# A two-expert mixture kernel's routing tables: one-hot tables for all eight experts, or for two with the rest scattered as 64-byte records

## The reference, cut to what matters

```python
logits = xf @ gate_w.T                       # xf: the rotated tokens, 4096 x 512
scores = softmax(logits); topv, topi = top_k(scores, 2)
gates = topv / topv.sum(-1)
# place of a token in its expert: running count over first choices, then second; valid below cap = 1024
flat_idx = where(valid, topi * cap + loc, 0)
disp[flat_idx] += xf * w                     # w = valid
h = relu(de @ fc1_w[e].T + fc1_b[e])         # 1024 x 512 by 512 x 2048, for each e
eo = h @ fc2_w[e] + fc2_b[e]                 # 1024 x 2048 by 2048 x 512
out = x + (eo[flat_idx] * gates * w).sum()   # over the two choices
```

## Time and profile before

| | |
|---|---|
| median of 3 runs | 1422.17 us (1420.65 to 1422.97) |
| the profiled execution's own time | 1426.31 us |
| its span in the trace | 1424.3 us |
| mean granted TensorE clock | 0.989 of full |
| PE busy | 1377.4 us, 97% of the span |
| DVE / ACT / POOL busy | 74% / 50% / 22% |

### The profile page before, as it was taken

One profiled execution on the slowest core, in us unless ns is written; L12 is line 12 of the kernel. 1 busy time (PEld: TensorE's weight loads), 2 busy tenths in 40 slices (PEclk: granted clock), 3 DMA queues, 4 the chain that ended last, 5 costly groups with the idle time before them and its releaser, 6 DMA issues.

```text
span 1424.3 us, 18010 instructions
## 1 busy us (share of the span) xinstructions
PE 1377.4 (97%) x6154; PEld 1129.6 (79%) x6154; DVE 1058.2 (74%) x1598; ACT 705.1 (50%) x1056; POOL 310.6 (22%) x322
## 2 busy tenths in 40 slices
PE   8488999999999999999999999999999999999997
PEld 5367888888888888888888888888888888888885
DVE  6897879686886778686896878777796868855443
ACT  5445445545464455554464445554455454644442
POOL 1054303321025202241033201251032200220021
PEclk9799999999999999999999999999999999999999
DMA  8666575566466564476466564575555533543232
GB/s 293 234 161 154 117 153 154 166 121 150 91 188 156 119 127 133 142 162 137 92 178 164 106 139 117 156 170 132 99 170 145 114 78 67 153 120 68 51 109 67
DMA packets 448684, 194.15 MB, mean 136 GB/s; under 512 B 398432, under 2 KB 400617, under 8 KB 446674
## 3 DMA queue, kind: packets, MB, share of 16 engines
q1 hardware_dynamic: 426466, 125.98, 40.0%
q0 software_dynamic: 22128, 67.03, 15.1%
HBM read 153.21 MB, written 39.98 MB: 136 GB/s over the span
## 4 chain that ended last, share of the span: by engine, by line
PE 93%; DVE 2%; ACT 1%; DMA 1%; issue 1%; POOL 1%; another core or an unknown queue 0%; SPq 0%; POOLq 0%; ACTq 0%
PE ps L1210 15%; PE ps L1206 15%; PE ps L1214 15%; PE ps L1181 14%; PE ps L1182 14%; PE ps L1183 14%; PE ps L1126 1%; PE ps L1198 1%; PE ps L1197 1%; PE ps L1199 1%; PE ps L1108 1%; PE ps L1109 1%; DMA x_all<-in_x 1%; POOL h L371 0%; DMA h<-in_x,gather_row 0%
## 5 line engine op out<-in xcount | busy, mean ns | idle before, releaser
L1181 PE MATMUL ps<-yc_hi,w1c_hi 128*128 128x512 f32 x896 | 350.2, 391 | 4.2 <-ACT s L606 2.2
L1182 PE MATMUL ps<-yc_lo,w1c_hi 128*128 128x512 f32 x896 | 349.4, 390 | 0.0
L1183 PE MATMUL ps<-yc_hi,w1c_lo 128*128 128x512 f32 x896 | 349.2, 390 | 0.0
L1206 PE MATMUL ps<-w_hi,h_hi 128*128 128x512 f32 x952 | 254.4, 389 | 0.0
L1210 PE MATMUL ps<-w_hi,h_lo 128*128 128x512 f32 x952 | 254.4, 389 | 0.0
L1214 PE MATMUL ps<-w_lo,h_hi 128*128 128x512 f32 x952 | 254.4, 389 | 0.0
L1206 PEld LDWEIGHTS ps<-w_hi,h_hi 128*128 128x128 f32 x952 | 178.7, 188 | 37.1
L1214 PEld LDWEIGHTS ps<-w_lo,h_hi 128*128 128x128 f32 x952 | 178.7, 188 | 37.1
L1210 PEld LDWEIGHTS ps<-w_hi,h_lo 128*128 128x128 f32 x952 | 178.7, 188 | 37.0
L1181 PEld LDWEIGHTS ps<-yc_hi,w1c_hi 128*128 128x128 f32 x896 | 168.5, 188 | 43.1 <-ACT s L606 2.6
L1183 PEld LDWEIGHTS ps<-yc_hi,w1c_lo 128*128 128x128 f32 x896 | 168.6, 188 | 35.2
(11 more groups left out here) (181 smaller groups left out, 1500.8 us busy)
## 6 DMA issues: line engine op xcount, KB each, us to landing
w_raw<-in_L_ffn_fc_w SPq DMA_DIRECT2D x232, 256.0 KB
w_raw<-in_L_ffn_fc_w SPq DMA_DIRECT2D x512, 64.0 KB
slots_dram<-x_blk POOLq DMA_DIRECT2D x28, 512.0 KB
x_blk<-slots_dram SPq DMA_DIRECT2D x224, 64.0 KB
out<-x_all SPq DMA_DIRECT2D x8, 1024.0 KB, 12.3
x_all<-in_x SPq DMA_DIRECT2D x7, 1024.0 KB, 13.3
b_bc<-in_L_ffn_fc_b POOLq DMA_DIRECT2D x8, 256.0 KB
x_all<-in_x SPq DMA_DIRECT2D x4, 256.0 KB, 4.1
```

Source lines behind the costliest of these rows:

```text
L1181: pe.matmul(bank, hi, yc_hi[:, y, q, :], start=first and q == 0, stop=False, skip_group_check=True)
L1182: pe.matmul(bank, hi, yc_lo[:, y, q, :], start=False, stop=False, skip_group_check=True)
L1183: ins = pe.matmul(bank, lo, yc_hi[:, y, q, :], start=False, stop=last and q == 1, skip_group_check=True)
L1206: pe.matmul(eo_s[:, b, :], h_hi[:, c, blk], w2_hi[:, w, :], start=False, stop=False, skip_group_check=True)
```

## The change

The tables of experts 0 and 1 alone (16 blocks, `NB` = 8 each) are still made by one-hot products, each expert in a product of its own: the slot number is cut the other way (place in the expert = 8 p + n), so that the block row is 8 wide (`hot_t0`, `hot_t1`) and the row of places 128 wide (`hot_b0` in four parts, `hot_b1` in two). `read_slots(0)` hands expert 0's indices to POOL before expert 1's table is finished.

For all slots token and gate go as a record of 64 bytes into a DRAM table of 8192 rows (`table_dram`), one indirect scatter of 128 records for each of the 64 columns of choices, at the row `slot_row`, which POOL computes (`finish_records`); then the first 8 bytes of each record are read back by eight DMAs (`table`), and DVE makes from `table` the gather rows of experts 2 to 7, `scatter_row` of all, and takes the gates from it (`read_table`). The softmax no longer stands between the logits and the two best experts: those are taken from the logits, and POOL subtracts and sums beside DVE. `gates_dram` and the 64 gathers of gates are gone.

POOL's queue is written anew, and so are the places of `cut_x` in the first expert and at the start of the second on SP, and one wait on SP holds the third load of first-layer weights until the eight blocks of expert 0 have landed. ACT and DVE wait for `records_ready` before the first group. The core of the diff:

```diff
@@ sync
             load_w1(1)
+            sp.wait_ge(x0_in[2 * SB - 1], 16)
             load_w1(2)
@@ gpsimd
+            pool.dma_start(table_dram.rearrange("(p k) a -> p (k a)", p=P), zeros[:, :]).then_inc(table_cleared, 16)
+            pool.wait_ge(masked, 1)
+            pool.tensor_tensor(dl[:, :, :], score[:, :, :], mx.unsqueeze(2).to_broadcast([P, TJ, E]), ALU.subtract
+                               ).then_inc(shifted, 1)
...
             pool.wait_ge(out_init, 16 * CHUNKS)
+            pool.wait_ge(table_cleared, 16)
+            pool.wait_ge(slots_ready, 2)
             gather_x(0)
+            finish_records()
+            store_x(0)
             load_b2(0)
             gather_x(1)
-            pool.wait_ge(gates_stored, 16)
-            gather_gates(0)
+            scatter_records(range(0, 4))
+            store_x(1)
+            scatter_records(range(4, 14))
+            gather_x(2)
+            scatter_records(range(14, 18))
+            store_x(2)
+            scatter_records(range(18, 22))
+            gather_x(3)
+            scatter_records(range(22, 26))
+            store_x(3)
+
+            for G in range(2, GROUPS):
+                pool.wait_ge(p6_done, G + 1)
+                scatter_records(range(26 + 6 * (G - 2), 26 + 6 * (G - 1)))
+            scatter_records(range(26 + 6 * (GROUPS - 2), TOPK * TJ))
+            pool.wait_ge(records_out, 16 * TOPK * TJ)
+            for e in range(E):
+                pool.dma_start(table[:, NB * e:NB * (e + 1), :],
+                               table_dram[CAP * e:CAP * (e + 1), 0:2].rearrange("(p n) a -> p n a", n=NB)).then_inc(table_in, 16)
             pool.wait_ge(y12_done, 2)
             gather_rows(0)
+            pool.wait_ge(tables_ready, 1)
@@ vector
+            def read_table():
+                after = slice(2 * NB, BLOCKS)
+                empty = slot_row[:, :].bitcast(F32)
+                dve.wait_ge(table_in, 16 * E)
+                dve.wait_ge(slots_ready, 2)
+                link(dve.tensor_scalar(empty, table[:, :, 0], 0.0, float(SKIP), ALU.is_equal, ALU.mult))
+                dve.tensor_scalar(gather_row[:, after], table[:, after, 0], -1.0, 0.0, ALU.add, ALU.max)
+                dve.scalar_tensor_tensor(scatter_row[:, :], table[:, :, 0], -1.0, empty, ALU.add, ALU.add
+                                         ).then_inc(tables_ready, 1)
...
+            block_table(0)
+            for part in range(4):
+                row_table(0, part, 4)
+            block_table(1)
+            row_table(1, 0, 2)
+            read_slots(0)
+            row_table(1, 1, 2)
             w1_low_parts(0, 1)
...
+                    if e == 0 and item == 2:
+                        read_table()
                     if item == 2:
                         add_rows(2 * e, (0, 1))
```

More of the change, by code:

```diff
@@ L86, in program @@
         scatter_row = sb("scatter_row", [P, BLOCKS], I32)
-        gate_row = sb("gate_row", [P, BLOCKS], I32)
-        gates = sb("gates", [P, BLOCKS])
-        gm = sb("gm", [P, TJ, E])
+        records = sb("records", [P, TOPK * TJ * 2 + RECORD])
+        slot_row = sb("slot_row", [P, TOPK * TJ], I32)
+        table = sb("table", [P, BLOCKS, 2])
         w1_raw = sb("w1_raw", [P, 2, D])
@@ new lines, in program @@
+        carry = sb("carry", [P, TOPK * E, TJ], where=early)
+        small = sb("small", [16, P], where=early)
+        b1_nat = sb("b1_nat", [E * HT, P], where=early)
+        before = sb("before", [P, P], where=early)
+        hot_b1 = sb("hot_b1", [P, TJ // 2, P, 2], BF16, where=early)
+        value = sb("value", [P, P, 2], BF16, where=early)
+        cnt = sb("cnt", [P, TOPK * E, TJ], where=early)
+        hot = sb("hot", [P, TOPK, E, TJ], where=early)
+        loc = sb("loc", [P, TOPK * E, TJ], where=early)
@@ L121, in program @@
         grot_hl = sb("grot_hl", [P, Q, 2 * E], F32R, where=early)
[L122 to L130, removed]
-        ones = sb("ones", [P, P], where=early)
[L132 to L157, removed]
+        ones = sb("ones", [P, P], where=early)
+        zeros = sb("zeros", [P, E * CAP * RECORD // P], where=early)
         early.close()
+        record_parts = records[:, 0:TOPK * TJ * 2].rearrange("p (k j a) -> p k j a", k=TOPK, a=2)
         yc_hi = sb("yc_hi", [P, 7, 2, SLAB], F32R)
@@ L332, in _ @@
                         load_w2(version(N) + 3)
-                    if e < E - 2 and tile == 11:
+                    if e == 0 and tile == 9:
+                        cut_x(4)
+                    if e == 0 and tile == 12:
+                        cut_x(5)
+                    if e and e < E - 2 and tile == 11:
                         cut_x(4 * e + 6)
@@ L448, in _ @@
                     gather_rows(2 * e + 2)
+                if e == 0:
+                    bring_x(6)
         @block.scalar
@@ L578, in _ @@
             y_high(0, T3, 3, y12)
+            act.wait_ge(records_ready, 1)
             for e in range(E):
@@ new lines, in _ @@
+            dve.tensor_copy(ahead[:, :], ahead_ps).then_inc(ahead_kept, 1)
+            link(first)
+            link(dve.tensor_tensor(loc01[:, :, :, :], loc01[:, :, :, :], hot[:, :, 0:2, :], ALU.mult))
+            link(dve.tensor_tensor(place01[:, :, :], loc01[:, 0, :, :], loc01[:, 1, :, :], ALU.add))
+            link(dve.scalar_tensor_tensor(place01[:, :, :], place01[:, :, :], float(CAP), place01[:, :, :], ALU.is_le, ALU.mult))
+            link(dve.tensor_scalar(place_i[:, :, :], place01[:, :, :], -1.0, None, ALU.add))
@@ L1143, in _, with find_tokens @@
             pe.matmul(ahead_ps[:, E:2 * E], ones[:, :], tot[:, 0:E], start=False, stop=True).then_inc(ahead_ready, 1)
-            for c in range(2 * TOPK):
-                pe.wait_ge(hots_ready, c + 1)
-                pe.wait_ge(hots_p_ready, c + 1)
-                for j in range(c % 2 * JH, (c % 2 + 1) * JH):
-                    ins = pe.matmul(token_ps, hot_b[:, c // 2, j // 2, :, j % 2], hot_q[:, c // 2, j // 2, :, :, j % 2],
-                                    start=(c == 0 and j == 0), stop=(c == 2 * TOPK - 1 and j == TJ - 1))
+            def find_tokens(k, parts, before_k):
+                hot_b, hot_q = ((hot_b0, hot_q0), (hot_b1, hot_q1))[k]
+                pe.wait_ge(hots_p_ready, k + 1)
+                for part in range(parts):
+                    pe.wait_ge(hots_ready, before_k + part + 1)
+                    for j in range(part * TJ // parts, (part + 1) * TJ // parts):
+                        ins = pe.matmul(token_ps[k], hot_b[:, j // 2, :, j % 2], hot_q[:, j // 2, :, :, j % 2],
+                                        start=(j == 0), stop=(j == TJ - 1))
                 ins.then_inc(hots_used, 1)
```

295 lines of the change are left out of this document (173 added, 122 removed).

## The result

The changed kernel takes 1428.86 us (median of 6 runs, 1426.93 to 1429.91), the kernel before, beside it, 1422.80 (6 runs, 1420.65 to 1423.72). The ratio is 1.0043 with a 95% interval of 1.0030 to 1.0056: slower by 0.4%, 1 us above the range's upper end and 11 us over the forecast. The profiled execution took 1428.87, its span is 1426.8.

What follows compares the result with a forecast made beforehand. PE bounds the kernel from 262 to 1390 us, the routing chain on DVE the front. Front -10, stop +5.2, slower clock +1 give -3.8 against the median 1422.2: 1418 us, range 1411 to 1428.

Steps and rivals of the forecast that it cites:

- Part 1: Front, two best experts taken without the softmax, POOL working beside DVE: gain 2.2 us.
- Part 2: Front, slot numbers: DVE's chain of 4.1 us shrinks to 2.1 with narrower instructions, gain 2.0 us.
- Part 3: Front, one-hot tables up to POOL's first gather of x: 11.6 us become 5.3, gain 6.3 us.
- Part 5: POOL's queue behind the gathers: the twelve operations of `finish_records` end near 83 us and cost 0.
- Part 4: From gathers to first products: rotation 9.4 us earlier, products 10 us earlier, with 8.5 and 11 as ends.
- The stop: PE's wait at the end of expert 0 for the `h_lo` behind late rows: 8t - 4.0, taken as 5.2 us.
- part 6: End of expert 0: scatters 1.4 us each, table reads t = 1.15 each, late rows; PE waits 5.2 us, plus 1.
- the clock: After PE's wait in expert 0 the next matmuls run slower for a while: 1 us added.
- part 7: Edits taken at no cost: `cut_x(3)` behind SP's weight loads, expert 0's second-half rows, gates' gathers gone.
- The gain is not there to spend: Rival: front gains 10 us, but expert 0's end is late too, 3 us more; 1421 to 1422 us, chance 0.13.
- cover: DVE's idle 2.23 us behind the turn at 182.15, said to hide most of the later `cut_x(3)`; otherwise 2 us.
- the line: Rival: table read price grows 0.15 us per 128 pieces, t = 1.65 to 1.75; 1423 to 1424 us, chance 0.20.

Runs made afterwards that it cites:

- the kernel with the hold taken away: Changed kernel, but DVE's subtractions and sums in tiles 5 to 11 of expert 0's second phase take one operand from PSUM (wrong results); 1416.80 us, ratio 0.9968.
- the kernels with DVE held: Kernel before, with DVE waiting in tile 3 of expert 0's second phase until PE's step 19, or step 18; 1428.41 and 1429.22 us.
- the kernel with the broken run: Changed kernel with one more DVE wait, in tile 6 of expert 0's second phase, for the landing of the gather of x (V = 5); 1419.46 us.
- the kernel with the rows early: Changed kernel with the four gathers of rows ahead of the last 38 scatters and the eight table reads; 1413.51 us, ratio 0.9940.

## Why the prediction was wrong

**What held.** Part 1: from the maximum of the logits to the scan took 8.20 us and takes 5.62 (46.39 to 52.01), gain 2.6 against 2.2. The dear end of this part, 1.3 us for POOL's operations beside DVE's, didn't come: the one of DVE's that stood beside POOL's subtraction (0.62 us at 49.53) took 0.50, the same one alone 0.42. Part 2: from the scan to the tables 6.73 and now 4.66, gain 2.1 against 2.0. Part 3: from the tables to POOL's first gather 11.64 and now 5.27, gain 6.4 against 6.3. Part 5: `finish_records` ran from 75.1 to 82.3 and nobody waited. The scatters took 1.16 + 0.30 us each, 1.4 forecast.

**Part 4 was too low.** The start of the rotation came 10.1 earlier against 9.4, but the first product 13.5 earlier, outside the 8.5 to 11 that the prediction itself set, and PE was 12.4 ahead at the end of p6 of G = 7 against 10. The term was 2.4 us too small; alone it would have made the kernel faster than forecast.

**The stop was smaller than forecast.** From p6 of G = 7 to DVE's first addition of rows 29.0 us went by, where the prediction's terms give 32.6. The scatters were dearer (11.8 us with POOL's start, 11.2 taken); all else was cheaper: landing 1.9 in place of 3.0, each table read 0.89 where 1.15 was taken, and the last gather's landing 3.1 in place of 4.0. The stop was 1.6 in place of 5.2. Had it been all, the time would have come out near or below the forecast: the kernel with the hold taken away ran 1416.8.

**The step that failed** is in part 6: "PE then stops for 232.2 + 8t + 2.0 - 238.2". It follows the late rows to the one `h_lo` for which PE asks next and ends there. It never asked what DVE does after it has stood, and what POOL has in its queue at that time. In before DVE idles 0.29 us in each tile:

```profile
238.02 0.69 DVE L940 SCALAR_TENSOR_TENSOR h_lo<-h,h_hi 128x512 fp32r<-128x512 f32 x1 [0.29 <-ACT h_hi L644]
```

There an issue of POOL that had begun at 236.60 ended at 238.61. Once late, DVE has no such idle time and works off its queue; the issue is held for 19.22 us, the bias behind it is late, and PE stops for 9.1 us and restarts at the lower clock. By the account above this took 9.2 + 2.4 + 2.2 = 13.8 us, by the kernel with the hold taken away 11; the sum had 1 us for it, the clock. The list of rivals had the two ends (part 7: "1 to 3 if POOL's issues are slower"; "The gain is not there to spend": 1421 to 1422), with issues of 2 us in mind, not of 19.

That the time came within 1 us of the range is luck. The range's upper end stood for table reads at 1.75 us each, and they took 0.89; the front's gain, 2.4 us more than taken, and the stop, 3.6 less, made up for part of what was missing.

The prediction had the rule at hand, and weighed it in part 1 only, at three small operations of the front. The Trainium skill (SBUF — State Buffer, "Who interferes with whom") says that a DVE operation with both inputs in SBUF contends with GpSimd's reads, and infers that it doesn't stop the writing of descriptors. The runs agree with both halves as far as they go: direct DMAs passed a gapless run at 0.6 to 0.7 us each, indirect ones were held. That an indirect issue is held because it reads its indices from SBUF is an inference from these two kinds, not shown by itself.

**Part 7** put `cut_x(3)` at no cost, or 2 us without its cover: PE waited 1.4 for it, and this wait is gone with the cut ahead of the weight loads. Why the cover, 2.23 us of idle DVE, didn't suffice wasn't looked into.

**The reference of the sum.** It set a difference worked out in one profiled execution against the median of others, 3.5 us faster. The first product came at 97.3, 95.3, 98.9 and 97.6 us in four profiles of kernels with before's front, and at 82.1 to 86.9 in nine with the new one: a front differs by 4 to 5 us from execution to execution, so that a gain read from one pair is good to some 4. The means, 97.3 and 84.1, are 13.2 apart, so that the 13.5 is no chance of this pair.

## What to carry to other kernels

When a change makes an engine wait, don't stop at the first consumer: ask what the engine does when it catches up, which idle moments that takes away, and which other engine lived on them. Then ask what stands behind a late issue in the same queue: here a bias of one row, which ACT needs early, was behind a gather that could wait. Keep POOL's indirect DMAs away from stretches in which DVE runs operations with two SBUF operands back to back for many tiles, or give DVE a wait there. An operand in PSUM in each of DVE's operations took the hold away too, but only in kernels that leave out the real operand, so it is no remedy that was tried. Gather early what doesn't depend on the slow step, here the rows, which never needed the table.

## What was not expected of the hardware

An indirect DMA's issue on POOL, mostly 0.95 to 1.2 us, took 19.22, 18.99, 18.99, 11.96, 4.37 and 3.92 us beside gapless DVE operations with two SBUF operands. Direct DMAs of POOL kept 0.6 to 0.8 us in such a run. With one operand in PSUM in all three operations of a tile no issue was held in those tiles, in two kernels.

What lets a held issue go is open in part. Three times (19.22, 11.96, 4.37) it ended 0.84 to 0.90 us behind the end of the operation after which DVE paused. In the kernels with DVE held (18.99 twice), and for the 3.92, it ended 0.94 to 0.96 behind the start of an `h_lo` ahead of which the trace shows no gap. All six ended at the same place of DVE's program: at the start of tile 13, whose `h_hi` is the first that ACT makes behind a copy of the bias; for the four longest that was 23.5 us behind the first addition of rows. In these last three cases ACT had ended that `h_hi` only 0.06 to 0.07 us before, so DVE may have waited for less than the trace resolves; this was not tested. It doesn't explain the gapless run that let one issue through per tile (2.0 us each, in the kernel with the broken run). Nor is every issue held: in the kernel with the rows early the second half of the gather (230.53, 0.97 us) went out wholly between two gaps of DVE, at 229.4 and 231.8.

A direct read of 1024 pieces of 8 bytes held POOL for 0.88 us, above the 0.61 for 128 pieces of 1 KB and far below the 1.65 of the line.
